# Masking the attention scores on TensorE instead of in VectorE's maximum, and one unrolled loop turned into a real one, in a four-layer network

## The reference

```python
scores = q @ k.T + bias                 # 256 x 256
scores = where(causal, scores, -inf)    # keys after the query are masked
probs = exp(scores - scores.max(-1)) / sum
out = probs @ v
```

## Time and profile before

| | us |
|---|---|
| median of 3 runs | 3442.44 |
| lowest and highest of them | 3431.8, 3455.69 |
| the profiled execution | 3431.8 |
| its span, first to last instruction | 3430.0 |
| PE busy | 2926.3 (85%) |
| DVE busy | 2336.1 (68%) |
| ACT busy | 1801.6 (53%) |

### The profile page before, as it was taken

The page is one execution under the profiler, slowest core; times in us unless marked ns, Lnnn a source line. Parts: engine busy times, 40 slices in busy tenths (PEclk is TensorE's granted clock), DMA queues, the critical chain, the costliest instruction groups (busy, mean ns, idle before and its releaser), DMA issues. The chain is left out here.

```text
span 3430.0 us, 71326 instructions
## 1 busy us (share of the span) xinstructions
PE 2926.3 (85%) x25734; PEld 2184.0 (64%) x25734; DVE 2336.1 (68%) x8754; ACT 1801.6 (53%) x3579; POOL 872.1 (25%) x878
## 2 busy tenths in 40 slices
PE   2766788888868999999999999999999766899975
PEld 2665556666635666666766666766666554799963
DVE  2554654444574577787777787777788456899998
ACT  0000334444422456655656655656655446788876
POOL 0000530000151121222222222222222228433367
PEclk9776699999976999999999999999999866999987
DMA  7001024433220000000000000000000001466621
GB/s 168 8 7 34 27 90 119 119 119 118 84 62 5 6 11 11 11 11 5 7 11 11 11 11 6 6 11 11 11 11 6 11 5 36 157 199 200 195 62 47
DMA packets 108203, 175.18 MB, mean 51 GB/s; under 512 B 17216, under 2 KB 78176, under 8 KB 107744
## 3 DMA queue, kind: packets, MB, share of 16 engines
q1 hardware_dynamic: 99680, 153.98, 15.4%
q0 software_dynamic: 8192, 16.79, 1.7%
HBM read 131.00 MB, written 26.74 MB: 46 GB/s over the span
## 5 line engine op out<-in xcount | busy, mean ns | idle before, releaser
L268 DVE CUSTOM_DVE_ANT_0 bank<-bank,masks 128x256 f32<-128x256 f32 (+1 forms) x1536 | 504.0, 390 | 152.9 <-PE bank L247 149.4
L247 PE MATMUL bank<-l_kT,l_qT 32*128 32x128 f32 (+1 forms) x3072 | 405.2, 358 | 7.0 <-DVE l_tops L268 2.9
L1975 ACT ACTIVATE l_probsT<-bank 128x768 f32<-128x768 f32 x256 | 207.8, 812 | 380.2 <-PE bank L247 379.2
L1948 POOL TENSOR_TENSOR l_rinv<-l_ssm,w_neg_half 128x8 f32<-128x8 f32 x128 | 209.8, 1639 | 675.2 <-DVE l_ssm L2216 675.1
L247 PE MATMUL bank<-l_qm,l_kT 32*128 32x128 f32 (+1 forms) x3072 | 379.7, 341 | 0.9 <-DVE l_qm L1309 0.9
L147 POOL TENSOR_TENSOR l_rstd<-l_var,w_neg_half 128x2 f32<-128x2 f32 (+1 forms) x58 | 43.3, 746 | 983.1 <-DVE l_var L142 983.1
L247 PEld LDWEIGHTS bank<-l_kT,l_qT 32*128 32x128 f32 x3072 | 227.0, 191 | 93.0 <-issue 51.4
L2587 DVE RECIPROCAL l_rden<-l_den 128x256 f32<-128x256 f32 x128 | 224.0, 1750 | 54.9 <-ACT l_den L2514 54.8
L247 PEld LDWEIGHTS bank<-l_qm,l_kT 32*128 32x128 f32 x3072 | 245.6, 191 | 20.2 <-issue 6.5
L828 POOL DMA_INDIRECT l_back<-sorted_y,l_pos x128 | 124.0, 968 | 497.1 <-DMA sorted_y<-l_y_tile 458.3
L268 DVE DVE_READ_ACCUMULATOR2_ANT l_tops<- 128x1 f32 x1536 | 217.5, 142 | 0.6
(11 more groups left out here) (340 smaller groups left out, 7697.6 us busy)
## 6 DMA issues: line engine op xcount, KB each, us to landing
l_expert<-in_experts SPq DMA_DIRECT2D x72, 768.0 KB, 4.0
l_expert<-in_experts SPq DMA_DIRECT2D x72, 578.0 KB, 3.5
l_x_tile<-sorted_x SPq DMA_DIRECT2D x144, 64.0 KB, 4.0
sorted_y<-l_y_tile SPq DMA_DIRECT2D x144, 64.0 KB, 3.6
l_v_half<-l_v SPq DMA_DIRECT2D x32, 264.0 KB, 3.1
sorted_x<-x_all SPq DMA_DIRECT2D x18, 256.0 KB, 3.9
l_v_half<-l_v SPq DMA_DIRECT2D x32, 132.0 KB, 3.1
x_all<-in_x SPq DMA_DIRECT2D x16, 128.0 KB
```

What stands on the lines that cost most here:

```text
L247: lasts.append(pe.matmul(bank[:, at:at + n * P], lhs[:, c * P:(c + 1) * P], rhs[:, x0 * P:(x0 + n) * P], start=not masked, stop=(i == 1 or ...
L268: last = dve.tensor_tensor_reduce(out=two[:, i, keys], in0=two[:, i, keys], in1=mask[:, keys], scale=1.0, scalar=NEG, op0=ALU.add, op1=ALU ...
L1948: pool.tensor_tensor(rinv[:, i, :], ssm[:, i, :], g.neg_half[:, 0:LH], ALU.pow).then_inc(rinv_ready[l], 1)
L1975: Bt.took(act.activation(probsT[:, (j // 2) % 2, 2 * (j % 2):2 * (j % 2) + 2, :], two[:, :, 0:AW], ACT.Exp), rd, use)
```

## The change

- `scores` in layers 1 and 2 calls `pe_masks_two` for ring A as well, ahead of the wait for ring B, with the mask that DVE used before. All jobs of `pe_rows` now add to a bank that holds a mask.
- `dve_max_two` becomes `dve_negmax_two`: two plain `tensor_reduce` in place of four `tensor_tensor_reduce`, one over 2 heads x 128 columns and one over 2 heads x 256. They give minus the maximum, and write no scores back.
- `queries_less_maxima` adds instead of subtracting. `tops` is named `negmax`.
- The 14 body rounds of layer 2 run as a real loop on each engine.

```diff
 def pe_rows(pe, jobs):
-        for bank, lhs, rhs, parts, masked in jobs:
+        for bank, lhs, rhs, parts in jobs:
             n, at, c, x0 = placed(parts)[i]
             lasts.append(pe.matmul(bank[:, at:at + n * P], lhs[:, c * P:(c + 1) * P], rhs[:, x0 * P:(x0 + n) * P],
-                                   start=not masked, stop=(i == 1 or not masked), skip_group_check=True))
+                                   start=False, stop=(i == 1), skip_group_check=True))
 
-def dve_max_two(dve, two, tops, way, mask):
-    for i in range(2):
-        for c, keys in enumerate((slice(0, way["split"]), slice(way["split"], AW))):
-            last = dve.tensor_tensor_reduce(out=two[:, i, keys], in0=two[:, i, keys], in1=mask[:, keys], scale=1.0,
-                                            scalar=NEG, op0=ALU.add, op1=ALU.max, accum_out=tops[:, c, i:i + 1])
-    return last
+def dve_negmax_two(dve, two, negmax, way):
+    s = way["split"]
+    dve.tensor_reduce(negmax[:, 0, :], two[:, :, 0:s], AX.X, ALU.max, negate=True)
+    return dve.tensor_reduce(negmax[:, 1, :], two[:, :, s:AW], AX.X, ALU.max, negate=True)
 
@@ layer 1, scores
                     two = A.fill(pe, n)
-                    jobs += [(two[:, i, :], qT[rows, b % 2, gi, :], kT[rows, b % 2, gi, :], FORWARD["parts"], False)
+                    pe_masks_two(pe, g, two, g.mask_causal)
+                    jobs += [(two[:, i, :], qT[rows, b % 2, gi, :], kT[rows, b % 2, gi, :], FORWARD["parts"])
@@ layer 1, queries_less_maxima
-                C.took(dve.tensor_tensor(qm[rows, place, :], qT[rows, of % 2, gi, :], b[rows, 0:S], ALU.subtract), ("maxima", n))
+                C.took(dve.tensor_tensor(qm[rows, place, :], b[rows, 0:S], qT[rows, of % 2, gi, :], ALU.add), ("maxima", n))
@@ layer 2, rounds
-            for it in range(2, B):
+            with looped(nc, eng, 2, B) as it:
                 one(("body", it))
@@ layer 2, scores
+                        pe_masks_two(pe, g, two, (g.mask_causal, g.mask_anti)[y])
```

More of the change, by code:

```diff
@@ L986, in layer1 @@
         vs = sb("vs", [P, 2, NC, NH, SLOT])
-        tops = sb("tops", [P, 2, NC, GH, SLOT])
+        negmax = sb("negmax", [P, 2, NC, GH, SLOT])
         probsT = sb("probsT", [P, 2, GH, AW])
@@ L1073, in scores @@
                     C.wait_taken(pe, ("maxima", n - 2))
-                    jobs += [(two[:, i, :], kT[rows, b % 2, gi, :], qm[rows, place, :], FORWARD["parts_t"], True)
+                    jobs += [(two[:, i, :], kT[rows, b % 2, gi, :], qm[rows, place, :], FORWARD["parts_t"])
                              for i, rows in enumerate(rows_of(n - 2))]
@@ L1086, in maxima @@
                 for c in range(NC):
-                    last = pe.transpose(b[:, c * P:(c + 1) * P], tops[:, n % 2, c, :, :].rearrange("p h s -> p (h s)"),
+                    last = pe.transpose(b[:, c * P:(c + 1) * P], negmax[:, n % 2, c, :, :].rearrange("p h s -> p (h s)"),
                                         g.ident[:, :])
@@ L1274, in _ @@
             stats_dve(dve, g, q, s, ch)
-            dve.memset(tops[:, :, :, :, :], 0.0)
+            dve.memset(negmax[:, :, :, :, :], 0.0)
             dve.memset(vs[:, :, :, :, :], 0.0).then_inc(setup_done, 1)
@@ L1302, in maxima @@
                 two = A.read(dve, n)
-                A.took(dve_max_two(dve, two, tops[:, n % 2, :, 2 * half:2 * half + 2, DH + 2], FORWARD, g.mask_causal), n)
+                A.took(dve_negmax_two(dve, two, negmax[:, n % 2, :, 2 * half:2 * half + 2, DH + 2], FORWARD), n)
             def queries_less_maxima(n):
@@ L1725, in scores @@
                         y, gi = u[1] // PAIRS, (u[1] % PAIRS) // 2
-                        jobs += [(two[:, i, :], qT[rows, y, gi, :], kT[rows, gi, :], (FORWARD, BACKWARD)[y]["parts"], False)
+                        pe_masks_two(pe, g, two, (g.mask_causal, g.mask_anti)[y])
+                        jobs += [(two[:, i, :], qT[rows, y, gi, :], kT[rows, gi, :], (FORWARD, BACKWARD)[y]["parts"])
                                  for i, rows in enumerate(rows_of(u[1]))]
@@ L1735, in scores @@
                         C.wait_taken(pe, rd, ("maxima", v[1]))
-                        jobs += [(two[:, i, :], kT[rows, gi, :], qm[rows, :], (FORWARD, BACKWARD)[y]["parts_t"], True)
+                        jobs += [(two[:, i, :], kT[rows, gi, :], qm[rows, :], (FORWARD, BACKWARD)[y]["parts_t"])
                                  for i, rows in enumerate(rows_of(v[1]))]
@@ L1805, in maxima @@
                                 last = pe.transpose(b[:, c * P:(c + 1) * P],
-                                                    tops[:, use[1] % 2, c, :, :].rearrange("p h s -> p (h s)"), g.ident[:, :])
+                                                    negmax[:, use[1] % 2, c, :, :].rearrange("p h s -> p (h s)"), g.ident[:, :])
                             C.filled(last, rd, use)
@@ L2105, in maxima @@
                                 y, h = use[1] // PAIRS, 2 * (use[1] % 2)
-                                A.took(dve_max_two(dve, two, tops[:, use[1] % 2, :, h:h + 2, DH + 2],
-                                                   (FORWARD, BACKWARD)[y], (g.mask_causal, g.mask_anti)[y]), rd, use)
+                                A.took(dve_negmax_two(dve, two, negmax[:, use[1] % 2, :, h:h + 2, DH + 2],
+                                                      (FORWARD, BACKWARD)[y]), rd, use)
                 def normalised(t):
@@ L2142, in queries_less_maxima @@
                             rows = slice(2 * SLOT * (j % 2), 2 * SLOT * (j % 2 + 1))
-                            C.took(dve.tensor_tensor(qm[rows, :], qT[rows, y, gi, :], b[rows, 0:S], ALU.subtract), rd, use)
+                            C.took(dve.tensor_tensor(qm[rows, :], b[rows, 0:S], qT[rows, y, gi, :], ALU.add), rd, use)
                 def shifted(t, b):
```

## The result

| | before | after |
|---|---|---|
| median (7 runs each) | 3439.14 | 3466.72 |
| lowest and highest | 3425.99, 3457.48 | 3462.66, 3477.81 |
| the profiled execution | 3431.8 | 3456.42 |
| its span | 3430.0 | 3454.6 |

The ratio is 1.0092, with an interval of 1.0064 to 1.012: 32 us longer by the ratio, 24.6 by the two profiled executions. By my bound of 1% the change is "no change that can be told", just: the forecast had put most of its chance on slower by over 1%.

The account below looks back on a forecast made before the run. PE was taken to bound layer 2, with layer 1 mixed. Masks +80.7, relief −25 in layer 1 and −11 in layer 2, loop +3 gave +47.7 us, so 3485 us, range 3448 to 3535.

Parts of the forecast that it names:

- masks, layer 1: PE in layer 1: mask matmuls for 128 more pairs at 0.21 us each, +26.9 us if nothing hides them.
- relief, layer 1: Layer 1: shorter maxima on DVE shorten PE's waits and give back 25 us of the 26.9.
- relief there: Layer 2: shorter waits for the maxima, 0.36 us once a round, and for `w_rot`, perhaps a third of its 0.4.
- the loop: Layer 2's 14 passes: branch cost taken as 3 us, register operations as nothing, with up to 20 kept for the range.
- the first two rounds: Start of layer 2, where PE isn't full yet: shorter waits give back perhaps 3 us.
- The maxima: DVE, each pair: two reductions take about 0.92 us in place of 1.23, a gain of 0.31.
- the shadow of `qm`: Layer 1: four masks fill about 0.1 us more of PE's wait for `qm`, in 26 cases, 3 us.
- three shortened waits: Layer 1, PE's waits: 9.4 us less for the maxima, 9.6 for the value product, 3 for the keys.
- The masks find room: Rival: new masks fit into PE's gaps or the wait for `qm`; +8 us, 3431.8 to 3450; chance 0.17.
- The likeliest: PE pays for the masks in layer 2 and layer 1 comes out even; 3465 to 3515 us; chance 0.65.
- Late fetch: Rival, layer 2's loop: code behind each back edge arrives late, 4.0 us a pass, 56 more, 3541; chance 0.13.
- DVE sets the pace: Rival, layer 1: every wait that DVE releases goes away, 84.8 us; −17 us, 3415; chance 0.05.

Follow-up runs that it names:

- e6: The change without its loop (layer 2 unrolled), with the four old masked maxima and the subtraction back on DVE while PE still writes the masks; 1.0169 of before.
- e2: The changed kernel without its loop: the 14 body rounds of layer 2 unrolled as before; 1.009 of before.
- e11: The kernel before, unrolled, with the whole new path (masks on PE, two reductions) only in the first two rounds of layer 2; 0.9958 of before.
- e9: The changed kernel with ring A's masks added twice in both layers; 1.031 of before.

## Why the prediction was right, and where it was not

Term by term, in us on the profiled execution; e6 separates masks from relief.

| term | predicted | measured |
|---|---|---|
| masks, layer 1 | +26.9 | +15.4 (about +20 at an equal clock) |
| relief, layer 1 | −25 | −16.1 (about −18 at an equal clock) |
| masks, 14 bodies of layer 2 | 14 × 16 × 0.21 = +47.0 | 14 × 3.13 = +43.8 |
| relief there | 14 × 0.5 = −7 | 14 × 0.22 = −3.1 |
| the loop | +3 | 14 × −0.12 = −1.7 |
| the first two rounds | 32 × 0.21 − 4 = +2.7 | −12.8 |
| all else | 0 | −1.1 |
| sum | +47.7 | +24.4 (24.6 by the spans; the rest is rounding) |

- **PE bounds layer 2, and the masks are paid there**: right. A round was forecast at 105.6 and lasts 105.48. The masks were sized right (0.196 to 0.218 a pair against 0.21), as was their change-over, paid once:

```profile
1878.09 0.60 PE L235 MATMUL bank<-masks,ident 128*128 128x256 bf16 x4
1878.62 0.49 PE L247 MATMUL bank<-l_kT,l_qT 32*128 32x128 f32 x4
```

  Four masks take 1878.62 − 1878.09 = 0.53 us to the first fp32 matmul; 0.52 was forecast from the earlier trace rows. The relief in a round was put too high, 0.5 for 0.22: it took 0.36 us off a wait for the maxima that is only 3.8 / 14 = 0.27 long, and 0.13 off the wait for `w_rot`. In after PE has no wait for the maxima left in these rounds, and the one for `w_rot` went from 5.4 us to 3.9, 0.11 a round. The price of the masks was too high by as much, 3.4 for 3.13. The round was right to 0.1 us partly because these cancel.
- **The maxima**: right. Two reductions occupy DVE for 1877.16 − 1876.22 = 0.94 us, against 1.23 in the earlier trace rows and 0.92 forecast:

```profile
1876.22 0.43 DVE L266 TENSOR_REDUCE l_negmax<-bank 128x2 f32<-128x256 f32 x1
1876.56 0.68 DVE L267 TENSOR_REDUCE l_negmax<-bank 128x2 f32<-128x512 f32 x1
1877.16 0.41 DVE L2142 TENSOR_TENSOR l_qm<-bank,l_qT 64x256 f32<-64x256 f32 x1
```

  The Trainium skill ("VectorE: DVE Perf Modes", rules for kernel authors) calls `tensor_reduce` on a hot path the slowest DVE operation and advises to consider restructuring. The form that it replaces here is slower still: measured, two reductions take 0.29 us less than the four fused ones for the same 768 elements a partition, and going from e6 to e2, which is only this step, brings 0.8% (1.0169 to 1.009).
- **Layer 1 comes out even**: right in the sum, +1.9 forecast, −0.7 measured, about +2 at an equal clock, but by two terms that are both too large. I gave only 3 us for the shadow of `qm` (they are within the −25), where the masks alone found 26.9 − 15.4 = 11.5 us of room, about 7 at an equal clock. And I added up three shortened waits as if none handed its time on. The waits for the maxima fell from 22.2 us in 26 cases to 17.1 in 20, a quarter, not a third.
- **The loop**: the mechanism (registers beside the work, branch reached by the hint) was right, the 3 us were not there. The price from layer 0's DVE has no bearing where DVE isn't last.
- **The first two rounds: the step that failed.** "The first rounds, where PE isn't full yet, perhaps 3" asked only how many waits would shrink there. The granted clock was in view, 0.77 from 1000 to 1200 us (0.87 between the first marks), and I did not ask what it would do when PE's work changes. I read rounds by their steady state from 1200 us on, where the clock is 1.00, and gave the one stretch with a low clock a guess. 15.5 of the 23 us between forecast and measured sum lie here, 4.7 in the loop, 2.6 in layer 1.
- **The rivals.** "The masks find room" gave +8 and the sum +47.7. The two profiles measured +24.6, a little nearer to the former, the ratio 32, nearer to the latter. Its mechanism isn't what happened: room was found for about a quarter of the masks in layer 1 and for almost none in layer 2. *The likeliest* gave 3465 to 3515, which holds the median. "Late fetch" is what happens without the hint. "DVE sets the pace": the waits that DVE releases in layer 1 went from 84.8 to 67.2 us, nothing like away.

## What to carry to other kernels

Moving work onto the engine that bounds a stage cost its full price here, however elegant; what is given to the relieved engine comes back only where that engine is waited for, so a mixed stage can take the same change for nothing. e11 keeps the old path in the rounds where PE is full and has the new one only at the start of layer 2, and it is the only version that is clear of before on the fast side. Most of its gain came with the granted clock, and what raised that isn't settled, so it is no rule. And before summing up terms, look at the granted clock of every stretch that the change touches: where it isn't 1.00, less gets done in the same time (119 matmuls against 202 in 20 us above), and here a small change in the work moved that by more than its own cost.

## What the runs showed of the hardware that I had not expected

- The clock at the start of layer 2: 53 us at the lower level before, 23 after, in two rounds with 64 matmuls more. It moved the time by 13 us in one pair of profiles, 10 on the mean of nine.
- A hole of some 4 us in PE's work at each back edge without the hint is followed by 13.7 us at the lower level: 10.4 us for a pass. The hint at the top of the loop brings the branch from 3.5 to 0.36 us.
- Some 100 register operations a pass on PE's queue, and 105.48 us a round with them, 105.60 without.
- The start varies: the first `qm` of layer 1 comes between 395.7 and 424.5 us in twelve profiles, though the code ahead of it is the same, and layer 1's own length by up to 6.7 us between kernels with the same code in it (612.2 to 618.9). Both go with the granted clock: 0.74 up to the first `qm` in before (397.0 us), 0.67 in e9 (424.5); and layer 1 takes some 0.23 us more for each us at the lower level. Much of the 1% by which two executions differ lies ahead of the stages that this change touches, so that marks inside a profile tell small changes better than the time of the whole.
